# Attention scores from keys and queries projected once per batch and spread by DMA, in an attention and expert kernel

## The reference, cut to what matters

```python
x = x + attn(layernorm(x), Wq, Wk, Wv, Wo)      # x: 16 batches x 256 tokens x 128
x = x + ffn(layernorm(x), gate_w, w1, w2)       # 8 experts, 64 tokens each
...
q = (x @ Wq).reshape(B, T, HEADS, D_K)          # 16 heads, D_K = 8, D_V = 64
k = (x @ Wk).reshape(B, T, HEADS, D_K)
v = (x @ Wv).reshape(B, T, HEADS, D_V)
scores = einsum('bhqd,bhkd->bhqk', q, k) / scale   # causal mask, softmax
out = einsum('bhqk,bhkd->bhqd', attn, v).reshape(B, T, HEADS * D_V) @ Wo
```

## Time and profile before

| | us |
|---|---|
| median of three runs | 667.4 |
| the profiled execution, its own time | 668.7 |
| its span | 666.7 |
| busy: TensorE, VectorE, ScalarE, GpSimd | 592.9, 432.1, 418.6, 350.7 |
| data moved by DMA, mean over the span | 18 GB/s |

### The profile page before, as it was taken

How to read it: one execution, slowest core, us unless ns; L and a number is a source line. 1 busy time by engine, 2 the same in 40 slices (tenths; PEclk the granted TensorE clock), 3 DMA queues, 4 the chain that set the end, 5 groups by cost and what they waited for, 6 DMA issues and landing times. The chain is left out here.

```text
span 666.7 us, 15350 instructions
## 1 busy us (share of the span) xinstructions
PE 592.9 (89%) x5252; PEld 486.0 (73%) x5252; DVE 432.1 (65%) x1073; ACT 418.6 (63%) x1418; POOL 350.7 (53%) x373
## 2 busy tenths in 40 slices
PE   1899999999999999999999999997418999999964
PEld 0577877878778787787777877766307989989863
DVE  3578787787887877878778787784474234433233
ACT  2599778787787877879778797782205444323320
POOL 4577677586776867767776677672330111011120
PEclk9999999999999999999999999999658999999995
DMA  9500000000000000000000000000001001000001
GB/s 272 177 2 2 0 2 1 1 2 1 2 0 0 0 0 0 0 0 0 0 0 0 0 0 1 1 0 1 1 32 49 17 18 32 13 13 18 17 17 40
DMA packets 13548, 12.28 MB, mean 18 GB/s; under 512 B 832, under 2 KB 10304, under 8 KB 13504
## 3 DMA queue, kind: packets, MB, share of 16 engines
q1 hardware_dynamic: 13504, 11.69, 5.9%
HBM read 9.57 MB, written 2.11 MB: 18 GB/s over the span
## 5 line engine op out<-in xcount | busy, mean ns | idle before, releaser
L340 ACT ACTIVATE prob<-s_ps,neg_max 128x128 f32<-128x128 f32 (+1 forms) x512 | 209.5, 431 | 28.3 <-DVE neg_max L457 20.3
L303 POOL TENSOR_TENSOR k_diag<-kT,own_block 128x512 fp32r<-128x512 f32 x64 | 66.6, 1041 | 115.9 <-DVE kT L452 114.7
L320 POOL TENSOR_TENSOR probn<-prob,inv 128x1024 f32<-128x1024 f32 x64 | 121.3, 1896 | 2.6 <-DVE inv L522 2.6
L340 ACT ACTIVATION_READ_ACCUMULATOR prob<-s_ps,neg_max 128x1 f32 x512 | 110.5, 216 | 0.0
L597 PE MATMUL ctx_ps<-probT,v_sb 128*64 128x256 f32 (+1 forms) x1024 | 97.3, 332 | 0.8 <-DVE probT L519 0.8
L786 POOL TENSOR_TENSOR y_parts<-y_sb,y_parts 128x512 fp32r<-128x512 f32 x16 | 20.9, 1304 | 140.5 <-ACT y_parts L802 140.5
L597 PEld LDWEIGHTS ctx_ps<-probT,v_sb 128*64 128x64 f32 x1024 | 63.5, 136 | 29.9 <-issue 11.5
L457 DVE TENSOR_REDUCE neg_max<-s_ps 128x4 f32<-128x1024 f32 x64 | 77.7, 1214 | 0.4 <-PE s_ps L563 0.3
L498 DVE TENSOR_REDUCE neg_max<-s_ps 128x4 f32<-128x512 f32 x64 | 44.0, 688 | 48.4 <-PE s_ps L621 48.4
L295 POOL TENSOR_TENSOR probn<-prob,inv 128x512 f32<-128x512 f32 x64 | 66.7, 1042 | 11.5 <-PE t_ps L614 11.5
L896 DVE TENSOR_TENSOR y_sb<-y_ps,slot_prob 128x512 f32<-128x512 f32 x16 | 11.1, 692 | 88.6 <-PE y_ps L974 88.6
(11 more groups left out here) (144 smaller groups left out, 1420.1 us busy)
## 6 DMA issues: line engine op xcount, KB each, us to landing
x_all<-in_L_attn_x SPq DMA_DIRECT2D x4, 512.0 KB, 6.9
w_raw<-in_L_ffn_w SPq DMA_DIRECT2D x1, 2048.0 KB, 11.8
toks<-tok_rows SPq DMA_DIRECT2D x8, 256.0 KB, 3.1
out<-x_all SPq DMA_DIRECT2D x16, 128.0 KB, 1.8
wv_raw<-in_L_attn_Wv SPq DMA_DIRECT2D x1, 512.0 KB, 5.0
wo_sb<-in_L_attn_Wo SPq DMA_DIRECT2D x1, 512.0 KB, 5.7
wqk_raw<-in_L_attn_Wq SPq DMA_DIRECT2D x1, 64.0 KB, 3.5
wqk_raw<-in_L_attn_Wk SPq DMA_DIRECT2D x1, 64.0 KB, 3.6
```

Source lines behind the costliest of these rows:

```text
L303: nc.gpsimd.tensor_tensor(k_diag0[r][:, :, :], bcast(f32(kT[r][:, 0:P]), 1, HG), bcast(own_block[:, :], 2, P), ALU.mult)
L320: nc.gpsimd.tensor_tensor(probn[r][:, HG * P:].rearrange("p (i k) -> p i k", i=HG), prob[r][:, HG * P:].rearrange("p (i k) -> p i k", i=HG ...
L340: last = nc.scalar.activation(prob[r][:, first + i * keys:first + (i + 1) * keys], scores[:, i, :], ACT.Exp, bias=neg_max[:, r, block_, i: ...
```

## The change

Queries and keys of a whole batch are projected at once, at j=0, from weights that are not spread. ScalarE rounds the product to `qk_hi`, VectorE writes the rest `qk_lo`. The DMA queue stores both to DRAM, eight stores of 128 KB per batch, so that the four row groups of each head lie there side by side, and loads them back as `qT` (512 KB) and into the diagonal blocks of `k_diag` (four loads of 128 KB). The rest of `k_diag` is zeroed once, at the start. The per-unit projection, qT, kT, k_diag0 and k_diag1 go. Score block 1 takes two matmuls of 512 columns in place of four of 256. The new projection stands on TensorE between the context and the values of step j=0; score block 0 of step j=2 waits for the loads. The transposes L644 move from j=0 to j=3 before, the first norm from j=0 to j=2 before, its statistics from j=2 to j=0 before, ahead of the copy of transposes of that step. The loads of x (parts 1 to 3), w1 and w2 move behind the loads of batch 0, of batch 1, and near the end of attention.

```diff
-        wqk_hi = sb("wqk_hi", [P, 2, H, 4, DK], F32R)
+        wqk_hi = sb("wqk_hi", [P, 2, H * DK], F32R)
...
+        QK_STORES = 16 * 8
+        QK_LOADS = 16 * (1 + HG)
...
+            for b in range(B):
+                sp.wait_ge(qk_hi_done, b + 1)
+                await_count(sp, qk_loaded, QK_LOADS * b)
+                for to, w, copies in ((q_rows, 0, (0, 1)), (k_rows, 1, (0, 2))):
+                    for copy in copies:
+                        sp.dma_start(to[:, copy, :, :], f32(qk_hi[:, w, :])).then_inc(qk_stored, 16)
+                sp.wait_ge(qk_lo_done, b + 1)
+                for to, w, copies in ((q_rows, 0, (2, 3)), (k_rows, 1, (1, 3))):
+                    for copy in copies:
+                        sp.dma_start(to[:, copy, :, :], f32(qk_lo[:, w, :])).then_inc(qk_stored, 16)
+                sp.wait_ge(qk_stored, QK_STORES * (b + 1))
+                if b == 0:
+                    sp.wait_ge(zeroed, RING)
+                await_count(sp, s1_done, G * (b - 1))
+                sp.dma_start(f32(qT[b % RING][:, :, :]),
+                             q_rows.rearrange("(j i) r d t -> (i r d) j t", j=G)).then_inc(qk_loaded, 16)
+                for i in range(HG):
+                    sp.dma_start(f32(k_diag[b % RING][i * ROWS:(i + 1) * ROWS, :, i, :]),
+                                 k_rows.rearrange("(j i) r d t -> i (r d) j t", j=G)[i]).then_inc(qk_loaded, 16)
...
-            pool.wait_ge(lows_ready, 3)
+            nc.gpsimd.memset(f32(k_diag[1][:, :, :, :]), 0.0).then_inc(zeroed, 1)
...
-                        pool.wait_ge(qk_ready, u + 3)
-                        await_count(pool, s1_done, u + 1)
-                        nc.gpsimd.tensor_tensor(k_diag0[r][:, :, :], bcast(f32(kT[r][:, 0:P]), 1, HG),
-                                                bcast(own_block[:, :], 2, P), ALU.mult)
-                        nc.gpsimd.tensor_tensor(k_diag1[r][:, :, :], bcast(f32(kT[r][:, P:T]), 1, 2),
-                                                bcast(own_half[:, :], 2, P), ALU.mult).then_inc(k_ready, 1)
-                    if j == 3 and has(b + 2, B):
+                    if j == 1 and has(b + 2, B):
                         pool.wait_ge(stats1, b + 3)
...
                     if has(u + 1, UNITS):
                         act.wait_ge(max1, u + 2)
                         exps(r1, 1, s1_ps, T, HG * P, exp1)
+                    if j == 0 and has(b + 1, B):
+                        act.wait_ge(qk_done, b + 2)
+                        await_count(act, qk_stored, QK_STORES * (b + 1))
+                        nc.scalar.activation(qk_hi[:, :, :], misc_ps[1][:, :].rearrange("p (a t) -> p a t", a=2),
+                                             ACT.Copy).then_inc(qk_hi_done, 1)
...
+            nc.vector.memset(f32(k_diag[0][:, :, :, :]), 0.0).then_inc(zeroed, 1)
...
                     if j == 0 and has(b + 1, B):
-                        dve.wait_ge(rstd1_done, b + 2)
-                        await_count(dve, xT_done, b + 1)
-                        norm(xn1, lambda tb: x_all[:, (b + 1) * TB + tb, :], mv1, rstd1, xn1_ready)
+                        dve.wait_ge(qk_hi_done, b + 2)
+                        nc.vector.tensor_tensor(qk_lo[:, :, :], extra[:, :].rearrange("p (a t) -> p a t", a=2),
+                                                f32(qk_hi[:, :, :]), ALU.subtract).then_inc(qk_lo_done, 1)
+                    if j == 2 and has(b + 2, B):
+                        dve.wait_ge(rstd1_done, b + 3)
+                        await_count(dve, xT_done, b + 2)
+                        norm(xn1, lambda tb: x_all[:, (b + 2) * TB + tb, :], mv1, rstd1, xn1_ready)
...
-                    if j == 2 and has(b + 2, B):
+                    if j == 0 and has(b + 2, B):
...
                         norm_stats(lambda tb: x_all[:, (b + 2) * TB + tb, :], bn6, mv1, bn1_done, b + 3, stats1)
...
                         for rows, i in tiles:
-                            nc.tensor.matmul(s1_ps[:, i:i + 2, 0:P], qT[r1][rows, P:T], k_diag0[r1][rows, i:i + 2, :],
+                            nc.tensor.matmul(s1_ps[:, i:i + 2, :], qT[kb][rows, q, P:T], k_diag[kb][rows, q, i:i + 2, :],
                                              start=True, stop=False, skip_group_check=True)
...
+                    if j == 0 and has(b + 1, B):
+                        pe.wait_ge(xT_ready, b + 2)
+                        for w in range(2):
+                            last = split_product(misc_ps[1][:, w * T:(w + 1) * T], wqk_hi[:, w, :], wqk_lo[:, w, :],
+                                                 xT_hi[1 - par][:, :], xT_lo[1 - par][:, :])
+                        last.then_inc(qk_done, 1)
...
-                        pe.wait_ge(k_ready, u + 3)
+                        q, kb = (j + 2) % G, par if j < 2 else 1 - par
+                        if j == 2:
+                            pe.wait_ge(qk_loaded, QK_LOADS * (b + 2))
...
-                    if j == 0 and has(b + 1, B):
-                        pe.wait_ge(xn1_ready, b + 2)
+                    extra = misc_ps[1]
+                    if j == 3 and has(b + 2, B):
+                        pe.wait_ge(xn1_ready, b + 3)
+                        await_count(pe, x1_ready, b if has(b - 1, B) else 0)
                         for tb in range(TB):
                             last = nc.tensor.transpose(extra[:, tb * P:(tb + 1) * P], xn1[:, tb, :], ident[:, :])
                         last.then_inc(xT_done, 1)
...
                     if j == 3 and has(b - 2, B):
                         pe.wait_ge(x2T_ready, b - 1)
+                        pe.wait_ge(v_ready, u + 3 if has(u + 2, UNITS) else UNITS)
```

More of the change, by code:

```diff
@@ L71, in block_kernel @@
         w1_raw = sb("w1_raw", [P, E, FF])
+        with nc.sbuf_tensor("k_diag_even", [P, G, HG, T], F32R) as k_diag_even:
+            pass
         w2_sb = sb("w2_sb", [P, E, HC, D])
@@ L137, in attention @@
         ctxT = [sb(f"ctxT{r}", [P, H * DV // P, T]) for r in range(RING)]
[L139 to L143, removed]
+        qk_hi = sb("qk_hi", [P, 2, T], F32R)
+        qk_lo = sb("qk_lo", [P, 2, T], F32R)
+        qT = [sb(f"qT{r}", [P, G, T], F32R) for r in range(RING)]
+        k_diag = [k_diag_even, sb("k_diag_odd", [P, G, HG, T], F32R)]
+        q_rows = nc.dram_tensor("q_rows", [H, 4, DK, T], F32).ap()
+        k_rows = nc.dram_tensor("k_rows", [H, 4, DK, T], F32).ap()
         neg_max = sb("neg_max", [P, RING, 2, HG])
@@ L180, in attention @@
         qk_hi_done = sem("qk_hi_done")
-        qk_ready = sem("qk_ready")
-        k_ready = sem("k_ready")
+        qk_lo_done = sem("qk_lo_done")
+        qk_stored = sem("qk_stored")
+        qk_loaded = sem("qk_loaded")
         v_done = sem("v_done")
@@ L235, in _ @@
             sp.dma_start(gate_sb[:, :], gate_w).then_inc(wo_loaded, 16)
[L236 to L239, removed]
+            for b in range(B):
[17 more added lines that the diff above has]
+                                 k_rows.rearrange("(j i) r d t -> i (r d) j t", j=G)[i]).then_inc(qk_loaded, 16)
+                if b == 0:
+                    for i in range(1, 4):
+                        part = slice(i * XPART * TB, (i + 1) * XPART * TB)
+                        sp.dma_start(x_all[:, part, :], x_tiles[:, part, :]).then_inc(x_loaded[i], 16)
+                if b == 1:
+                    sp.dma_start(w1_raw[:, :, :], w1.rearrange("e c h -> c e h")).then_inc(experts_loaded, 16)
+            sp.wait_ge(s1_done, G * (B - 1))
             sp.dma_start(w2_sb[:, :, :, :], w2.rearrange("e (k p) c -> p e k c", p=P)).then_inc(experts_loaded, 16)
@@ L348, in batch @@
                     r1, r2, rm = (j + 1) % RING, j % RING, (j + 1) % RING
[L349 to L354, removed]
+                    if j == 0 and has(b + 1, B):
+                        act.wait_ge(xT_done, b + 2)
+                        nc.scalar.activation(xT_hi[1 - par][:, :], misc_ps[1][:, 0:T], ACT.Copy).then_inc(xT_hi_done, 1)
                     if has(u + 1, UNITS):
@@ L400, in _ @@
[L400 to L406, removed]
@@ L415, in _ @@
-            dve.wait_ge(w_lo, 2)
-            for w in range(2):
-                nc.vector.tensor_copy(wqk_lo[:, w, :, 1:4, :], bcast(f32(wqk_lo[:, w, :, 0, :]), 2, 3)).then_inc(w_lo, 1)
+            nc.vector.memset(f32(k_diag[0][:, :, :, :]), 0.0).then_inc(zeroed, 1)
+            dve.wait_ge(w_hi, 2)
+            nc.vector.scalar_tensor_tensor(out=wqk_lo[:, 0, :], in0=wqk_raw[:, 0, :], scalar=DK ** -0.5,
+                                           in1=f32(wqk_hi[:, 0, :]), op0=ALU.mult, op1=ALU.subtract).then_inc(w_lo, 1)
@@ L463, in batch @@
                         nc.vector.tensor_copy(gate_logit[:, bass.ds((b - 3) * TB, TB), :],
-                                              extra[:, 0:TB * E].rearrange("p (t e) -> p t e", t=TB)).then_inc(gate_ready, 1)
-                    if j == 1 and has(b + 1, B):
+                                              misc_ps[0][:, 0:TB * E].rearrange("p (t e) -> p t e", t=TB)).then_inc(gate_ready, 1)
```

(9 more changed lines are left out.)

92 lines of the change are left out of this document (20 added, 72 removed).

## The result

The changed kernel takes 706.8 us in the median of four runs (700.9 to 712.4) against 667.6. The slowest of the four ran in a slower state of the chip, at a lower clock; the other three have a median of 706.0, and by them the kernel takes 1.055 times as long, with a 95% interval of 1.048 to 1.062. The forecast was 656 and the range ended at 679.

A forecast was written before the change was run, and what follows sets the result against it. TensorE was taken to set the pace, VectorE's copy just behind it. From 668.7 us, 17.6 less over 16 batches and 6 more at the start gave 657.1, or 656 against the median; range 637 to 679.

The forecast's parts named there:

- TensorE's saving: Projection on TensorE: six matmuls a batch where there were 24, 2.16 us a batch less; score block 1 taken as 0.
- what VectorE gives back: TensorE's transposes wait for VectorE's copy: 1.1 us a batch gained, not 2.2; causal masks 5.99, 5.28, 8.44, 6.72 us apart.
- The wait behind mask 0: After step 0's causal mask, TensorE's second transposes wait 1.22 us for VectorE's copy, which stands behind the first norm's statistics.
- Rival A: VectorE doesn't give it back: TensorE keeps 2.16 us and the norm's 0.6 a batch, 630 us; it or half: 0.17.
- D: Score block 1 on TensorE: pairs of 512 columns cost more than four of 256; 8 us, 664 us; chance 0.06.
- The DMA round trip: Stores and loads end 9.9 us behind step 0's mask, needed at 11.0 by score block 0 of step 2: cost nothing.
- Rival B: Trip too late for score block 0 of step 2: loads land at 12.5, 1.5 us late, 679 us; chance 0.17.
- The price of a late trip: At score block 0 of step 2, each us the loads are late costs a us on TensorE, 15 times.
- The start: Before the steady part: first score block moves from 18.93 to 27.5 us, partly given back; net +6 us, bounds +3 and +9.
- Rival C: Second norm on VectorE collides with GpSimd's multiplication: the 0.6 us wait stays and grows, some 10 us, 666 us; chance 0.12.

The follow-up runs named there:

- the loads freed: Changed kernel, but from batch 1 on the loads read batch 0's rows, issued ahead of the stores, which go to other tensors: 659.0 us, 0.986 of before.
- The kernel with the filled wait: Changed kernel with eight extra matmuls of 512 columns, results overwritten, on TensorE just ahead of its wait for the loads: 697.6 us.
- the run with the statistics last: Changed kernel with the first norm's statistics moved behind VectorE's copy of transposes in step 0: 707.0 us.

## Why the prediction was wrong, point by point

- **TensorE's saving, and what VectorE gives back: right.** 5.99, 5.28, 8.44 and 6.72 were forecast; with the loads freed they are 6.03, 5.29, 8.45 and 6.72. The wait behind mask 0 is there, and moving the statistics takes 0.7 off it. Rival A falls, and so does D: the pairs of 512 columns cost nothing extra.
- **The DMA round trip: the step that failed.** I made the trip 9.9 us against a need of 11.0 and cost it at nothing; it took 13.1, and the cover of 1.1 us was not there. "A store of 128 KB takes 0.38 us to issue" was read from stores that go out one at a time, 7 us apart in the mean (16 from 557.1 to 664.5). In a row of eight they take 0.62 each, so the last one was issued 1.9 us later. Landing took 2.4 us instead of 1.8. The trace counts landing from the start of the issue and I had counted it from the end, which takes 0.3 off the error. The loads took 6.7 us instead of 5.7 from the first issue to the last landing: the last of the five is issued 1.9 us after the first (225.66 against 223.74) and lands 4.8 later, and I had left these issues out. Store issue and landing were taken at the value of a DMA that runs alone.
- **Rival B had the place right and the cause wrong.** It had the stores land after 4.4 us; they landed after 2.4. Its 12.5 us for the trip lies near the 13.1 by luck: what made the trip late was mostly the issue on the queue, as the run with four stores shows. The 2.3 us that the prediction worked out for a store from the Trainium skill, DMA: Bandwidth & Descriptors, was the better size; the section it cites gives its 2.0 us for DMAs that GpSimd issues, and the 2.4 here is measured on the SP queue.
- **The price of a late trip: a term was missing.** Rival B had a us on TensorE for each us late. TensorE waited 2.1 us in the mean over batches 1 to 14, and mask 1 to mask 2 came out at 7.66 instead of 5.28: 14 x 2.4 = 33 us over the forecast. I had not looked at what TensorE's clock does behind such a wait: 1.6 us in seven of the 14 batches, 0.8 in the mean, 11 us. The kernel with the filled wait gave back 9.
- **The start: +6 forecast.** The first mask moved from 19.53 to 31.02, 11.5 us, since the trip there has the same error, 3 us. The second unit gave 2.2 back, as forecast (the first two masks are 3.57 us apart, before 5.81), and by mask 1 of batch 0 the kernel was 8.3 behind (44.82 against 36.51). Then the trip of the second batch came too late as well: 12.1 behind at mask 2 (54.64 against 42.58), 6 more than forecast.
- **Sum.** The other two intervals came out 0.1 us a batch under the forecast, 2 us. 656 + 33 + 11 - 2 + 6 = 704, measured 706.8.
- **Rival C** did not occur in the changed kernel (0.34 us an instruction), as forecast; it occurred as soon as the statistics were moved, by the mechanism given.

## What to carry to other kernels

A chain of small DMAs is priced by its issues on the queue as well as by its bytes: count the issues, take the issue and landing times of DMAs that follow each other closely, and merge stores first, because a store of 256 KB cost the queue no more than one of 128 KB here. A wait that a hand-ordered kernel hides with a margin of a us must be costed as if it could be missed, and a miss on TensorE can cost more than its own length: behind half of the waits here the clock fell too. When a wait on one engine is taken away, look at once for what now stands beside what: here a freed VectorE ran its norm beside GpSimd's multiplication.

## What the runs showed of the hardware

- Eight stores of 128 KB to DRAM in a row occupy the SP queue 0.62 us each and land after 2.4 us; single ones took 0.38 and 1.8. A store of 256 KB took 0.38 to 0.62 as well, the first of a row the 0.38, and landed after 2.2 to 2.8. Why a store in a row costs more than one alone stays open.
- A store of 1 MB to DRAM and its load back took 13.5 us in thirteen DMAs (216.91 to 230.46) and at most 11.0 in nine (first issue at 196.51, last load issued at 202.9 and landed within 4.6).
- Waits of TensorE of 1.6 to 3.9 us are followed by a long stage in half of the batches of the changed kernel (granted clock 0.83 in the one read) and by a short one in the others (1.00). In this trace and that of the run with the statistics last, over batches 1 to 14, none of the 13 waits up to 1.78 us had a long stage behind it, and 12 of the 15 longer ones had. Why not the other three stays open.
- Two VectorE instructions of the norm took 0.59 us alone and 1.88 to 2.48 beside a GpSimd multiplication of 1.9. The Trainium skill, GPSIMD Engine Reference, key points, says that the two share their SBUF interfaces; these are the sizes here.
- 2 MB of DMA traffic a batch did not slow TensorE's step: with the loads freed, all four intervals are within 0.04 us of those worked out from the kernel before.
